# Score maxima of the second attention: two chunks on the two row halves of the array

## The reference

```python
q_hk = (hidden_q @ Wq.T).reshape(Bv, Sv, H, K)
q_big = jnp.einsum('bshk,hkq->bshq', q_hk, w_kc_q)
q_big = _apply_rope(q_big, sin_q[None, :, None, :], cos_q[None, :, None, :])
kv_r = _apply_rope(kv_c, sin_k[None], cos_k[None])
q_r = jnp.einsum('bshq,hqr->bhsr', q_big, W_qr)
k_r = jnp.einsum('bld,hdr->bhlr', kv_r, W_kr)
scores = jnp.einsum('bhsr,bhlr->bhsl', q_r, k_r)
attn = jax.nn.softmax(scores, axis=-1)
ctx_c = jnp.einsum('bhsl,bld->bhsd', attn, kv_r)
```

## Time and profile before

| | us |
|---|---|
| median of 3 runs | 853.45 (852.42 to 854.16) |
| profiled execution | 848.99 |
| its span | 847.2 |
| TensorE busy | 794.6 (94%) |
| VectorE busy | 583.1 (69%) |
| GpSimd busy | 465.7 (55%) |
| ScalarE busy | 379.0 (45%) |
| mean granted TensorE clock | 0.991 |

### The profile page before, as it was taken

How to read it: one execution, slowest core, us unless ns; L and a number is a source line. 1 busy time by engine, 2 the same in 40 slices (tenths; PEclk the granted TensorE clock), 3 DMA queues, 4 the chain that set the end, 5 groups by cost and what they waited for, 6 DMA issues and landing times.

```text
span 847.2 us, 15449 instructions
## 1 busy us (share of the span) xinstructions
PE 794.6 (94%) x5802; PEld 586.9 (69%) x5802; DVE 583.1 (69%) x1149; ACT 379.0 (45%) x845; POOL 465.7 (55%) x474
## 2 busy tenths in 40 slices
PE   8888899999887999999999999999999999999886
PEld 6667758999665677776776677676776767766445
DVE  4688653323686756778787887888779778786545
ACT  3367422222303545544554554554465365454531
POOL 3112148000502878768777777777767775568630
PEclk9999999999999999999999999999999999999998
DMA  8731237895101000000000000000000000000000
GB/s 299 250 139 51 71 114 297 316 352 214 52 1 38 1 5 26 11 2 28 11 2 12 23 11 11 25 11 1 17 27 1 11 7 10 3 14 11 10 7 10
DMA packets 21897, 53.04 MB, mean 63 GB/s; under 512 B 7482, under 2 KB 15940, under 8 KB 19392
## 3 DMA queue, kind: packets, MB, share of 16 engines
q1 hardware_dynamic: 20800, 50.42, 17.6%
q0 software_dynamic: 1024, 1.64, 0.7%
HBM read 45.80 MB, written 5.36 MB: 60 GB/s over the span
## 4 chain that ended last, share of the span: by engine, by line
PE 69%; DVE 16%; ACT 6%; issue 5%; DMA 3%; SPq 1%; POOL 0%; POOLq 0%; ACTq 0%; DVEq 0%
PE ps L1174 15%; PE ps L1186 12%; PE ps L1154 7%; PE ps L1091 6%; PE ps L1035 4%; PE ps L1096 3%; PE ps L1119 3%; PE ps L1211 3%; PE ps L1048 2%; DVE nm L1937 2%; DMA xs<-xs_scratch 2%; PE ps L987 2%; DVE xyz L1908 2%; DVE sm L1723 2%; ACT pt L1624 1%
## 5 line engine op out<-in xcount | busy, mean ns | idle before, releaser
L627 POOL TENSOR_TENSOR acc<-acc,pt 120x800 f32<-120x800 f32 (+1 forms) x157 | 297.6, 1895 | 83.6 <-ACT pt L1624 48.9
L1624 ACT ACTIVATE pt<-ps 120x400 f32<-120x400 f32 (+1 forms) x384 | 189.8, 505 | 211.9 <-PE ps L1174 201.3
L1937 DVE TENSOR_REDUCE nm<-ps 128x1 f32<-128x482 f32 (+1 forms) x336 | 212.5, 656 | 93.9 <-PE ps L1154 89.5
L1174 PE MATMUL ps<-qh,khl 128*120 128x400 f32 (+1 forms) x384 | 157.1, 409 | 10.8 <-ACT pt L1624 7.8
L1186 PE MATMUL ps<-pt,kv 120*64 120x400 f32 (+1 forms) x768 | 143.9, 510 | 0.0
L1154 PE MATMUL ps<-khl,qh 128*128 128x482 f32 (+1 forms) x336 | 131.1, 392 | 5.6 <-DVE nm L1937 4.7
L1174 PE MATMUL ps<-ql,kh 65*120 65x400 f32 (+1 forms) x384 | 133.5, 348 | 0.0
L1174 PEld LDWEIGHTS ps<-qh,khl 128*120 128x120 f32 (+1 forms) x384 | 70.3, 183 | 58.6 <-issue 32.2
L1186 PEld LDWEIGHTS ps<-pt,kv 120*64 120x64 f32 (+1 forms) x768 | 50.4, 137 | 63.1 <-issue 52.8
L1174 PEld LDWEIGHTS ps<-ql,kh 65*120 65x120 f32 (+1 forms) x384 | 70.7, 184 | 5.3
L1091 PEld LDWEIGHTS ps<-x3T,wqb 128*128 128x128 f32 x512 | 67.2, 194 | 6.6 <-DVE xyz L1908 4.3
(11 more groups left out here) (260 smaller groups left out, 1206.9 us busy)
## 6 DMA issues: line engine op xcount, KB each, us to landing
ew<-in_expert_w_dram SPq DMA_DIRECT2D x14, 1536.0 KB, 7.1
fw<-in_ternary_w_dram SPq DMA_DIRECT2D x6, 512.0 KB, 7.4
spread<-inv_scratch SPq DMA_DIRECT2D x30, 100.0 KB, 2.7
craw<-in_ctx_dram SPq DMA_DIRECT2D x8, 360.0 KB
woT<-in_wo_t_dram SPq DMA_DIRECT2D x1, 2048.0 KB, 15.3
xs_scratch<-zero SPq DMA_DIRECT2D x1, 1792.0 KB, 8.7
xs<-xs_scratch SPq DMA_DIRECT2D x14, 128.0 KB, 6.8
ys_scratch<-ysb SPq DMA_DIRECT2D x14, 128.0 KB, 6.7
```

The lines of the kernel that those rows point to most:

```text
L627: nc.gpsimd.tensor_tensor(total[r, :, :], before[r, :, :], pt[j % PT_BUF][r, :, :], ALU.add).then_inc(p_added, 1)
L1174: last = mm(ps[0:key_rows(t), k % 2, 0:HT], lhs[:, keys], rhs[:, HT * a:HT * a + HT], start=first, stop=not first)
L1624: nc.scalar.activation(pt[j % PT_BUF][0:rows, k % 2, :], ps[0:rows, k % 2, 0:HT], ACT.Exp).then_inc(p_ready, 1)
L1937: nc.vector.tensor_reduce(nm3[0:w, i, n:n + 1], ps[0:w, 3 + m % 2, 0:MN], AX.X, ALU.max).then_inc(m_reduced, 1)
```

## The change

Chunks no longer multiply by low and high parts over 128 rows, but by the high part alone over 64 rows. An even chunk takes `kh1` and `qh` on rows 0 to 63, an odd chunk the same numbers from `khl` and `qh` on rows 64 to 127. In the slot loop the two chunks of slots `at` and `at + 1` now both stand in slot `at`, for odd `at`; chunk 20 has no partner. The two banks, the waits of a chunk, and the order on VectorE, ScalarE, GpSimd and SyncE are the same. The maxima leave the low part of the keys out.

```diff
@@ max_chunk
                 i, n = c // 3, c % 3
                 w = m_rows(i)
-                mm(ps[0:w, 3 + m % 2, 0:MN], qh[u % 2][:, 128 * i:128 * i + w], khl[b % 2][:, MSTART[n]:MSTART[n] + MN],
+                high = kh1[b % 2] if c % 2 == 0 else khl[b % 2]
+                r = slice(CD * (c % 2), CD * (c % 2) + CD)
+                mm(ps[0:w, 3 + m % 2, 0:MN], qh[u % 2][r, 128 * i:128 * i + w], high[r, MSTART[n]:MSTART[n] + MN],
                    start=True, stop=True).then_inc(m_done, 1)
@@ the slot loop of TensorE
                     scores(k)
-                    if u + 1 < NU and MAX_FROM <= at < MAX_FROM + MC:
-                        max_chunk(u + 1, at - MAX_FROM)
+                    if u + 1 < NU and MAX_FROM <= at < MAX_FROM + MC and (at - MAX_FROM) % 2 == 0:
+                        for c in range(at - MAX_FROM, min(at - MAX_FROM + 2, MC)):
+                            max_chunk(u + 1, c)
```

## The result

The changed kernel took 913.57 us in the median of four runs (910.89 to 923.96), the kernel before on the same chip 852.93 (851.04 to 854.16). The ratio is 1.0745, with a 95% interval from 1.0707 to 1.0784. The forecast was slower, 889 us, with 878 to 899 from its own bounds. The direction held, the size did not: +61 us by the medians, +65.7 by the profiled spans (912.9 against 847.2), where +36 was forecast.

What follows compares the result with a forecast made beforehand. TensorE's instruction stream, 94% busy, was taken as the bound. Mode changes 24.2 us, first set 2 and waits 10 summed to 36, added to the median 853.45 for 889 us; own range 878 to 899, wider range 866 to 915.

Steps and rivals of the forecast that it cites:

- scores to pair / pair to the next: TensorE in the slot loop: 0.27 us from last score matmul to the pair, 0.41 from pair to what follows.
- changes of mode per set: Switching between 64-row pairs and neighbouring matmuls adds 1.61 us per set of 21 chunks, 24.2 us over 15 sets.
- first set: Chunks ahead of the slot loop, 238 to 261 us, woven with projections: 2 us added, bounds 0 and 3.
- The price of one change of mode: On TensorE at each switch: about 0.09 us empty, plus 0.10 for weights not loaded ahead (0.08 into a projection).
- three neighbouring places of the trace before: L769 to L778, L1186 to L1174, and L1001: sources of the 0.09 or 0.10 empty and 0.10 or 0.08 weights prices.
- Rival 1: Pairs stream side by side and no change of mode is paid: 829 us, chance 0.07.
- rival 2: The engine empties at a change of mode, but weights come in meanwhile: 858 us, chance 0.08.
- rival 3: The mode is paid and a pair's chunks do not run side by side: 35 us more, 915 us, chance 0.08.
- Chunk 20: Slot 21: the chunk without partner pays both changes of mode, +0.38 us a set.
- The wait: A pair's second chunk waits for VectorE's reductions: slot 9 7 us, slots 17 and 3 3.5 each; taken 10, bounds 2, 18.
- The six chunks that stand alone: First set, each between two projection parts: 0.36 us each, 0.09 hidden in VectorE's wait, so 6 x 0.27 = 1.6 us.
- the wide range of 866 to 915: Range in us leaving out rival 1, rival 2 and the upper half of rival 3.

Runs made afterwards that it cites:

- the second profile of this kernel: The changed kernel run again with nothing altered, beside the kernel with slot 9's wait filled by spare matmuls: 920.64 us, ratio 1.0676 to the kernel before.

## Why the forecast was right and wrong

By its own steps, from the profiled executions (span +65.7 us):

| | forecast | measured |
|---|---|---|
| scores to pair / pair to the next | 0.27 / 0.41 | 0.278 / 0.416 |
| start of one partner to the other, no wait | up to 0.01 | 0.003 to 0.004 |
| changes of mode per set | 1.61 | 1.05 to 1.35 |
| loop without the clock: modes and waits | 24.2 + 10 = 34.2 | 32.6 |
| first set | 2 | 2.2 up to its thirteenth chunk |
| clock | 0 | 27.7 (with the modes of the last eight chunks of the first set) |
| stages ahead of the first chunk | 0 | 2.9 |

**The price of one change of mode was right.** The engine empties for about 0.09 us at each change, and the weights behind it lie open for about 0.10. The three neighbouring places of the trace before gave the price of a pair to 0.01 us. The Trainium skill's rule in "TensorEngine Tiling (Array Packing)", section Key Properties, that a change of the tiling mode drains the engine, is borne out: 0.28 instead of 0.18 at each pair. Rival 1 and rival 2 fail on that row and on the loads at 595.08, rival 3 on the 3 ns between partners. Why the loads are held back is not shown. That a pair and the score matmul before it share rows is no reason by itself: in the ordinary stream the load at 508.85 lies beside a running matmul on the same rows.

**Chunk 20 was oversized.** It was to cost 0.38 a set; taking its changes of mode away gave at most 0.1. The step that failed is "chunk 20 pays both changes": the one behind lies beside the reduction, the join and the transpose that end the set. 1.61 less 0.30 is 1.31, inside what was measured.

**The wait was right in kind and in its main place, a little small.** The second chunk of slot 9 comes 1.47 behind its partner, in six units where seven were counted; slot 3 is late as forecast, slot 17 by half of it, and slots 15 and 19 are late unforecast. A first unit of a batch became 2.9 us longer and a second one 1.4. With 1.2 for the modes in each (the middle of the two measured prices) that leaves 1.7 and 0.2 for waits and for standing together, so some 13 over seven batches where 10 was taken, inside the bounds of 2 and 18. The quiet increase of the loop is 29.5 in units 1 to 15 (45.3 in all, less 15.8 of clock, below) and 3.1 in unit 0 (taken from unit 2 of the second profile of this kernel, 38.7 against 35.6). The two misses, modes too dear and waits too cheap, nearly cancelled.

**The step that failed is the clock, a term that was put at nothing.** The sum took every row at full clock, because the earlier trace rows show 1.00, and nothing in it asked whether the changed stream would keep that. It did not:
- First set: up to its thirteenth chunk it took 14.3 us against 12.1 before, the forecast's 2. The six chunks that stand alone follow each other at 1.03 us instead of 0.67, the whole 0.36 and not the 0.27 that was taken. From 255.3 on it ran at half clock, 20.7 us against 14.9: 5.8. The changes of mode of the last eight chunks lie in these 5.8 and can't be told apart from the clock.
- Unit 0: half clock until 292.8, and 6.8 us more from 309.9. It is 9.2 longer, of which 3.1 are put down to modes and waits: 6.1. (The 3.1 are those of unit 2, with a wait in slot 9 that unit 0 does not have, so the clock's part may be up to 1 us more.)
- Units 2, 6 and 10: 1.6, 5.5 and 7.2. The last unit, which makes no chunks: 1.5 (6.8 us of half clock, 3.4 before; whether the change is behind it is not shown). Together 15.8.

That is 27.7 us. With 32.6 + 2.2 it makes 62.5, and 2.9 more passed before the first chunk (0.3 of the 65.7 is rounding and the tail). That last part is no effect of the change: this start lay between 238.1 and 245.3 us in the profiles of kernels that are the same up to there.

The measured 913.6 us lies near the 915 of rival 3 and inside the wide range of 866 to 915. That is luck: the chunks did run side by side, and what filled the gap was the clock, which no rival had.

What makes the clock fall in units 2 to 13 was told apart as far as one profile of each kernel goes. Without the idle time of slot 9 there is no fall, whether the wait is taken away (reductions in pairs) or filled (matmuls nobody reads). The other executions agree: their mean clocks are 0.966 to 0.975 and 0.959 to 0.979, while the eight of the changed kernel have 0.832 to 0.959. With the idle time and full rows there was no fall in the profile. With the row halves and no such wait, two of 3.4 us. With both, in three profiles, three, three and five falls behind the six waits, for 3.4 to 17.1 us. So the long falls were seen with both together alone; the one execution of the full-row pairs at clock 0.982 keeps it from being certain that they need both. Units 0, 14 and 15 follow no such rule: they have falls of 6.8 us without a wait in slot 9.

At the loop's start, where the first set has full rows, a fall comes with another wait, the 2.97 us for the row of maxima, which the kernel before has too. How long the half clock lasts there depends on the chunks behind it: 3.4 us before, 3.4 and 6.8 (with 3.4 more later) with full rows in pairs, 20.5 in both profiles with row halves in pairs.

**Open.** Why one slot 9 ends in a fall and the next, the same to 0.02 us in its rows, does not. Why the clock of the first set falls at 255 with row halves; TensorE had just stood idle for 0.55 us for a reduction, 0.18 before. Which property of the row-half stream keeps the clock down was not tried apart: it has more empty stretches, and fewer matmuls that use all 128 rows.

No version beat the kernel before. The best, full rows with the reductions in pairs, is 0.4% slower.

## What to carry to other kernels

Two small matmuls on two parts of the array do run side by side, but a group of them between full-array matmuls costs two changes of mode, 0.38 us here, against 0.21 saved by each pair. By these two numbers, an estimate, it takes at least two pairs in a row to win, with the banks for all of them free at once; no run tried that. Pulling two steps of a producer together takes the slack out of the ring between it and its consumer; the order on the consumer has to be changed with it, which by itself gave 26 us of the 61 back (887.5 against 913.6). And where a change adds idle time or empty stretches to TensorE's stream, price the clock too: where a fall of 13.7 us followed, one idle microsecond here cost 5.5 more, and filling it with useless matmuls was a gain.

## What was not expected of the hardware

- A wait of 1 us (0.98 idle) in the stream of row-half chunks was followed, 0.4 to 2.0 us behind the late chunk, by 3.4 to 17.1 us at the 1.2 GHz level, in 11 of 18 places of the same shape in three profiles. With full-row chunks a like idle time (1.16 us) was followed by none in the profile's six places.
- The half clock at the loop's start, at the same wait of 2.97 us, lasted 3.4 us in front of full-row chunks and 20.5 in front of row-half pairs.
- At the half clock a chunk on 64 rows takes 0.77 us instead of 0.48, and a unit in which it holds for 13.7 us loses 5.5 of the 6.9 that it could.
